# Layer 2's attention: the value products of two steps issued next to each other, in four column tiles

## The reference

```python
Q, K, V = (proj(Wq, bq), proj(Wk, bk), proj(Wv, bv))      # 16 heads of 8
logits = jnp.einsum('bhqd,bhkd->bhqk', Q, K) / scale
attn = jax.nn.softmax(logits * scale_matrix, axis=-1)
out = jnp.einsum('bhqk,bhkd->bhqd', attn, V)
out = out.transpose(0, 2, 1, 3).reshape(B, S, d) @ Wo.T + bo
```

## Time and profile before

| what | value |
|---|---|
| median of 3 runs | 5166.75 us (5161.05 to 5176.02) |
| the profiled execution's own time | 5168.04 us |
| its span | 5166.7 us |
| busy in the span | PE 4541.0, DVE 3154.0, ACT 2497.4, POOL 2316.0 us |
| mean granted TensorE clock | 0.944 |

### The profile page before, as it was taken

One profiled execution on the slowest core, in us unless ns is written; L12 is line 12 of the kernel. 1 busy time (PEld: TensorE's weight loads), 2 busy tenths in 40 slices (PEclk: granted clock), 3 DMA queues, 4 the chain that ended last, 5 costly groups with the idle time before them and its releaser, 6 DMA issues. The chain is left out here.

```text
span 5166.7 us, 68811 instructions
## 1 busy us (share of the span) xinstructions
PE 4541.0 (88%) x27376; PEld 2213.2 (43%) x27376; DVE 3154.0 (61%) x4176; ACT 2497.4 (48%) x3813; POOL 2316.0 (45%) x1323
## 2 busy tenths in 40 slices
PE   5999999987886777868799999987799999999997
PEld 3444444445654333323322222223455555555554
DVE  4656565636666777762377777844465655566563
ACT  2344444446663555542256666651244444444443
POOL 0455555558771677870100000000166666666674
PEclk8999999989997999989799999997899999999998
DMA  0000000011110000000000000000000000000000
GB/s 32 3 3 3 3 3 3 3 33 29 37 26 12 2 2 2 1 1 23 3 2 2 1 2 1 1 3 6 10 3 3 3 1 3 3 3 1 3 1 9
DMA packets 61954, 36.81 MB, mean 7 GB/s; under 512 B 36308, under 2 KB 53888, under 8 KB 61376
## 3 DMA queue, kind: packets, MB, share of 16 engines
q1 hardware_dynamic: 61632, 32.41, 2.5%
HBM read 22.03 MB, written 1.05 MB: 4 GB/s over the span
## 5 line engine op out<-in xcount | busy, mean ns | idle before, releaser
L793 DVE TENSOR_REDUCE L_part<-banks 128x2 f32<-128x1024 f32 (+2 forms) x1600 | 1882.2, 1190 | 988.1 <-PE banks L644 847.7
L778 ACT ACTIVATE L_weights<-banks 128x1024 f32<-128x1024 f32 (+1 forms) x1600 | 1579.8, 1000 | 1048.3 <-PE banks L676 835.6
L702 PE MATMUL banks<-L_weights,L_V 128*32 128x512 f32 (+3 forms) x6400 | 1497.3, 603 | 5.6 <-ACT L_weights L778 3.6
L1000 POOL TENSOR_TENSOR L_wsum<-L_wsum,L_weights 128x1024 f32<-128x1024 f32 (+1 forms) x448 | 983.4, 2195 | 55.8 <-ACT L_weights L778 3.1
L983 POOL TENSOR_TENSOR L_wsum<-L_wsum,L_two 128x1024 f32<-128x1024 f32 x240 | 570.3, 2376 | 854.9 <-DVE L_two L967 852.6
L702 PEld LDWEIGHTS banks<-L_weights,L_V 128*64 128x64 f32 (+1 forms) x6400 | 283.3, 123 | 459.4 <-issue 396.9
L676 PE MATMUL banks<-L_QH,L_KH 64*128 64x512 f32 (+3 forms) x1664 | 431.7, 453 | 18.1 <-issue 10.2
L2510 POOL MEMSET F_xr<- 128x16 f32 x1 | 0.1, 126 | 934.6 <-POOLq L97 934.6
L644 PE MATMUL banks<-L_KH,L_QH 64*128 64x512 f32 (+3 forms) x1664 | 371.1, 428 | 31.6 <-ACT L_weights L778 17.5
L676 PE MATMUL banks<-L_QL,L_KH 64*128 64x512 f32 (+3 forms) x1664 | 371.8, 382 | 0.0
L676 PE MATMUL banks<-L_QM,L_onesrow 64*128 64x512 f32 (+3 forms) x1664 | 371.1, 380 | 0.0
(11 more groups left out here) (446 smaller groups left out, 5914.3 us busy)
## 6 DMA issues: line engine op xcount, KB each, us to landing
F_early<-F_V SPq DMA_DIRECT2D x63, 128.0 KB, 2.3
F_tab<-xpos SPq DMA_DIRECT2D x8, 512.0 KB, 4.5
F_h<-L_ffn_h_w SPq DMA_DIRECT2D x2, 1024.0 KB, 8.1
F_wqkv<-L_ffn_wqkv SPq DMA_DIRECT2D x2, 768.0 KB
L_cos<-rope_cos SPq DMA_DIRECT2D x1, 1024.0 KB, 5.0
L_sin<-rope_sin SPq DMA_DIRECT2D x1, 1024.0 KB, 7.0
out<-X SPq DMA_DIRECT2D x1, 1024.0 KB, 5.1
F_z<-F_x SPq DMA_DIRECT2D x32, 31.8 KB
```

Source lines behind the costliest of these rows:

```text
L702: mm = pe.e.matmul(O[r, c:BANK], self.V[g % 2][:, kt, h, :], self.W[x % self.NW][:, y, c:BANK], start=kt < starts, stop=kt >= tiles - starts)
L778: act.e.activation(self.W[x % self.NW][:, :, c:BANK], self.banks(it)[:, :, c:BANK], ACT.Exp, scale=self.scale).then_inc(self.exped, 1)
L793: dve.e.tensor_reduce(self.part[n % 3][:, pr, j, p, :], self.banks(it)[:, :, 0:wide], AX.X, ALU.max).then_inc(self.mx_read, 1)
L1000: pool.e.tensor_tensor(acc[:, :, c:BANK], acc[:, :, c:BANK], W[:, :, c:BANK], ALU.add).then_inc(self.summed, 1)
```

## The change

The class of layer 2's attention no longer sets `APART`. It inherits `APART = False` from `Attention`, so `plan` takes its other branch for this layer: the round becomes scores x+2, the first half of the pieces, values x, values x+1, a single extra, scores x+3, the other pieces. The four value products of a round then stand next to each other, in four column tiles. Nothing else is edited.

```diff
 class NarrowAttention(Attention):
-    APART = True
     FREED = {"straight": "act", "v": "act", "den": "dve", "back": "act", "join": "dve", "shift": "dve", "arrive": "dve"}
     row = [0, 32, 64, 96]
```

## The result

The kernel after the change took 5356.07 us (median of 4 runs, 5328.39 to 5376.98) against 5171.39 us (5161.05 to 5177.38) for the kernel before on the same chip: a ratio of 1.036, interval 1.030 to 1.041. It is slower by 185 us, 6 us beyond the top of the predicted range.

What follows compares the result with a forecast made beforehand. Prediction: a latency chain through scores, exponential, bank pair, piece and values bounds layer 2's attention. Terms +4 +23 +19 +12 = +58 us on 5168.0 gave 5226, rounded down to 5215; range 5155 to 5350.

Steps and rivals of the forecast that it cites:

- the chain: Layer 2's attention round: scores, exponential, bank pair, piece, values, scores; 3.03 us before, 3.04 after, +4 us in all.
- the clock's term: Layer 2's attention: TensorE's new idle time lowers its clock part of the time; +23, +19 and +12 us, bounds 0 to +365.
- Value products together: Layer 2's attention: eight value matmuls take 1.00 us against 0.99 for four, so one 0.99 us group per round vanishes.
- The rival that has TensorE's work as the bound: Layer 2's first piece could precede the exponential's end; 0.4 us gained in each of 240 rounds, 5072 us; chance 0.10.
- VectorE, ScalarE, DMAs, projections, chunk ends: Layer 2's other work: stays covered or keeps its distances, projection rounds 4.90 us again; 0 us, chunk ends within 4 us.
- The last chunk: Layer 2's 16 rounds without pieces: expected at the low clock nearly throughout, 3.77 us against 2.82, about +12 us.
- the other case: Last chunk if the clock holds: 2.61 us a round against 2.82, -3 us over 16 rounds.
- layer 1's 12% low: Layer 2's ordinary and denominator rounds: low-clock share taken from layer 1, 77 of 638 us, +23 us.
- a third low: Layer 2's 38 projection and V rounds: a third of their 186 us at the low clock, 62 us, +19 us.
- the main case: Layer 2's attention: loop kept, clock low part of the time, 5190 to 5270 us, taken at 5215; chance 0.53.
- the second rival: Layer 2's attention: after the first projections the low clock may keep itself up, +180 to +365 us; chance 0.18.
- half-low case: Layer 2's attention at the low clock for half of the stage: +180 us, 5350 us.

Runs made afterwards that it cites:

- the pieces behind: Changed kernel with each round's first pieces moved from ahead of the values to behind them and the extra: 5485.11 us, ratio 1.061.
- the copies' run: Changed kernel with only ScalarE's order altered, the exponential ahead of the projection's two copies: 5190.17 us; ten runs, six at 5178 to 5191, four at 5235 to 5238.
- all other rounds filled: Changed kernel plus two zero-weight matmuls in every round that gets fillers, except the 26 with a K or Q projection: 5226.83 us, ratio 1.0114.

## Why the prediction was wrong

The direction, the chain and nearly all terms held; the size of the clock's term failed.

- *The bound.* Right. The chain was predicted at 3.04 us a round and is 3.05, and moving its links moves it as computed (3.24 with the pieces behind, 3.27 expected).
- *Value products together.* Right: 1.00 us for eight, as in layer 1. The rival that has TensorE's work as the bound (5072) is ruled out by the 0.72 us that TensorE waits in each ordinary round at full clock.
- *VectorE, ScalarE, DMAs, projections, chunk ends.* Right at nothing or nearly: projection rounds in a bunch 4.91 for 4.90, the two rounds of a chunk start 0.22 more at the full clock (12 of them, 3 us, inside the 4 us allowed), the other stages within 2 us.
- *The last chunk.* Wrong in sign. I had it low nearly throughout, +12 us. Its rounds are at the full clock and take 2.60 us each (2.61 computed), which is the -3 of the other case.
- *The clock's term.* This is the step that failed: "with layer 1's 12% low, 77 us, +23" for ordinary rounds, and "a third low, 62 us, +19" for those with a projection or a V product. Counted in the trace from the value products of one round to those of the next, 361 us of 750 in ordinary and denominator rounds were low, 85 of 158 in projection rounds and 74 of 75 in V rounds. With 0.32, the loss of a low ordinary round, taken for all, that is +116 where I had +23, and +51 where I had +19. With +4 and -3 the terms make 168 us, against 160 measured. The stage's clock, 0.75, lies below the 0.8 to 0.95 that was to be the sign of the main case.

What happened is thus the second rival, "the clock falls and stays", which I had at 0.18 and whose half-low case was computed at 5350. It should have been the forecast. Layer 1's share was the wrong proxy: in the 250 us read there the clock falls six times and is back after 3.4 or 6.8 us each time, so 12% is what short falls cost. I had the row that spoke against it, 40 us at 0.50 beside 72% busy TensorE, and used it for the rival only. The question for the sum was not how often the clock falls but whether the rounds that follow a fall can raise it. The low round also was too short by 0.17 us (4.33 for 4.50): piece to values is 0.72 at the low clock, not the 0.56 read where the clock was about to rise.

The Trainium skill ("TensorE: Matmul & The Clock Gate", A second HAM failure mode: psum-queue depth-cycling) describes a kernel whose matmul groups idle briefly while they cycle through PSUM banks, and whose clock then swings between the levels. The runs here agree, and add how unevenly: the same ordinary round, with its wait of 0.72 us, costs nothing while the clock is up, and can go on at the low clock for 235 us once a 1.7 us hole has brought it down.

Open: what decides whether a fall lasts 3 us or 235 us. Runs of one program differ in it (0.898 to 0.885 here, the two groups of the copies' run), so a part lies outside the order of the instructions. Nor is it shown why the clock differs behind the stage between kernels whose code there is the same.

## What to carry to other kernels

Before taking work off an engine that is 98% busy, follow the ring of buffers around one round: if a chain of latencies is just as long, the freed time becomes a wait. On TensorE that wait is not free. Compute what a round would cost at the low clock and ask whether such rounds, after a fall, would bring the clock back; if it is not clear that they would, take the low clock for a good part of the stage. The freed time is worth something only when other work is moved into it, as the projections were here (5356 us to 5130, with 5171 for the kernel before; about half of the last 42 came from the new place of the projections alone).

## What was unexpected of the hardware

- The clock has a memory at equal work. Beside ordinary rounds it stayed full with TensorE 77% busy, and among mostly ordinary rounds it stayed low for 235 us with TensorE 85% busy.
- Short waits start a fall. With all other rounds filled, one wait of 1.70 to 1.79 us was enough, 11 times. A row of ordinary rounds with 1.09 us in each 3.24 us did it once; with 0.72 us in each 3.05 us no trace shows it.
- Multiplications by zero weights, whose result is thrown into a sum as zero, hold the clock (1.00 in the stage) as well as useful ones and made this kernel 173 us faster.
